# Two attentions, the coupling networks and the flag branch in one program without barriers

## The chip, the cores and the metric

The kernel runs on one core of a Trainium2 chip. Five engines work side by side, each on its own stream of instructions: TensorE (PE, matrix products; its weight loads are listed as PEld), VectorE (DVE), ScalarE (ACT), GpSimd (POOL) and SyncE (SP, which here only issues DMAs). They wait for each other by counting semaphores. The metric is the time of one execution on the device, in microseconds (us); less is better.

## The reference

The input is 4 batches of 1024 tokens with 128 channels. Two layers are computed, each as `x = x + s * silu(g)` on the normalized x. In the first, s is a full attention with 16 heads of 8 channels and g a spiking feed-forward. In the second, s is a causal attention with ALiBi slopes, and g comes from small coupling networks that are applied in three cycles:

```
def _L1_ffn_ref(x, ...):
    gf = _global_net(x.mean(axis=1, keepdims=True), ...)
    out = x
    for _ in range(NUM_CYCLES):                  # 3
        tf = _coupling_net(out, ...)             # 128 -> 128 -> 64 -> 32 -> 1, gelu between, sigmoid at the end
        combined = 0.7 * gf + 0.3 * tf
        coupling = BASE_COUPLING + adaptive_range * (combined - 0.5) * 2.0
        out = out + coupling * _twist(out)
    return out

xn = _layernorm(x)
s = _L1_attn_ref(xn, ...)                        # causal, 16 heads, softmax(q k / sqrt(8) + alibi)
g = _silu(_L1_ffn_ref(xn, ...))
x = x + s * g
```

## The kernel before

**Stages.** `build` calls five stages one after the other: `prologue`, `row_maxima(0)`, `first_attention`, `middle`, `row_maxima(1)`, `second_attention`. Each is a block of its own: at its end every engine drains and meets the others at a barrier, and only then does an engine start on the next block. The blocks also own their tiles: each attention allocates its ring of four tiles `probs` and its PSUM banks (three slots of two banks for scores, one bank `o_ps` for the output, one bank `side`), and `middle` its hidden layers `h1`, `h2`, `h3`, `th` and two groups of four banks, pa and pb.

**The attentions.** A step is 512 queries by 128 keys of four heads. PE makes scores in two units of 128x1024, ACT takes the exponential of each unit into the ring, POOL masks the diagonal pieces (second attention only), and PE multiplies the ring's tile with the values `vt` into `o_ps`. Steps run in pairs. The order on each engine is written out by hand. Between the pairs PE does side work in the bank `side` (a "fill"), by a table: `side_fills` for the first attention and `second_fills` for the second. The second attention has 18 steps for each of 4 batches.

**`middle`.** It runs the coupling networks on all four batches, in two streams (0: batches 0 and 1; 1: batches 2 and 3) that take turns: round n belongs to stream n % 2, and there are six rounds, 0 to 5. In a round PE computes a layer, ACT its Gelu, four layers long; ACT ends with two Tanh (`couple`), and DVE with two twists, `twist(n, 0)` and `twist(n, 1)`, one for each batch of the stream. A twist is three instructions on 1024 columns (two on 64 partitions each, L1517, and one on 128, L1520). In each pass of the loop DVE does `twist(n - 2, 1)` and `twist(n - 1, 0)`. Twist (3,1) below is `twist(3, 1)`.

`middle` also finishes what the first attention left of batch 3, half 1 (the last 512 tokens). In round 0 PE projects the attention's output (L1654), DVE adds and multiplies it (`mix`, L1541) and normalizes (up to L816), PE turns it (L1632). In round 5, the last one, its q and k are projected (L1636, `rows_of`), ACT and DVE split them into a high and a low part, PE makes its v (L1640, `values`), and POOL, PE and DVE its norms (`norm_peak`). From the norms DVE makes `flag`, which says whether scores can grow so large that row maxima are needed. `row_maxima(1)` loads it on SP, PE and DVE (L682, L706, L729) and branches; with these inputs the flag is 0 and the long branch isn't taken.

**Around the seams.** ACT loads its Gelu table at the first instruction of `middle` (L1446) and the Exp table at the last (L1477). DVE clears `o_ps` at the start of each attention, and PE waits for this before its first scores.

## Time and profile before

| | us |
|---|---|
| median of 3 runs | 916.91 (916.01 to 917.1) |
| the profiled execution | 914.3 |
| its span | 912.6 |
| ACT busy | 829.2 (91%) |
| PE busy | 780.9 (86%) |
| DVE busy | 395.0 (43%) |
| POOL busy | 210.3 (23%) |

The span goes from the first to the last instruction of the profiled execution; about 1.7 us lie around it. Instructions are named by their line in the kernel, their engine and the tiles that they write and read. "Idle before, releaser" is the time for which an engine stood still before an instruction, and the engine and line that ended the wait; a name with a q at its end, as PEq, is the engine's sequencer, which handles waits, branches and barriers.

### The profile page before, as it was taken

The numbers are of one execution on the slowest core, as the hardware profiler recorded it, in microseconds if no ns is written. First come the engines' busy times: TensorE is split into PE (matmuls) and PEld (weight loads), VectorE is DVE, ScalarE is ACT, GpSimd is POOL, SyncE is SP. The second block draws the span as 40 slices with busy tenths as digits, with TensorE's granted clock in tenths as the row PEclk, the third lists the DMA queues.
The fourth block names the chain that finished last, engine by engine and source line by source line (L and its number), as shares of the span: only waits on it lengthen the run. The fifth ranks groups of instructions, "written<-read, shape, count | busy, mean of one in ns | idle before, by whom it ended". The sixth has DMA issues, their size and how long they took to land. (4 is left out here: it accounts for less than half of the span.)

```text
span 912.6 us, 22160 instructions
## 1 busy us (share of the span) xinstructions
PE 780.9 (86%) x9374; PEld 305.5 (33%) x9374; DVE 395.0 (43%) x862; ACT 829.2 (91%) x919; POOL 210.3 (23%) x259
## 2 busy tenths in 40 slices
PE   3949999899999999998999988755887878878876
PEld 2412434234343343433334333212332323323322
DVE  7821254443747446474444777881120121121122
ACT  7759999999999999999999956656999999999996
POOL 2201110130202212121311112002234334324333
PEclk9969999999999999999999999986999999999999
DMA  6882020200300202103000034010112022022000
GB/s 181 281 280 38 2 75 3 74 2 3 98 25 18 104 2 75 48 2 121 2 2 24 25 90 168 0 47 1 38 38 86 14 74 86 1 87 86 2 13 24
DMA packets 31948, 53.45 MB, mean 59 GB/s; under 512 B 5480, under 2 KB 16360, under 8 KB 31848
## 3 DMA queue, kind: packets, MB, share of 16 engines
q1 hardware_dynamic: 31848, 52.01, 18.2%
q8 instruction: 75, 1.23, 0.6%
q14 instruction: 25, 0.20, 0.1%
HBM read 31.29 MB, written 20.71 MB: 57 GB/s over the span
## 5 line engine op out<-in xcount | busy, mean ns | idle before, releaser
L979 ACT ACTIVATE a_probs<-a_sc 128x1024 f32<-128x1024 f32 x512 | 473.6, 1035 | 10.0 <-PE a_sc L1178 9.7
L1846 ACT ACTIVATE a_probs<-a_sc 128x1024 f32<-128x1024 f32 x288 | 269.6, 1047 | 21.6 <-PE a_sc L1997 17.1
L1193 PE MATMUL a_o<-a_probs,vt 128*18 128x256 f32 (+1 forms) x3072 | 271.3, 456 | 0.0
L1178 PE MATMUL a_sc<-q_st,k_st 32*128 32x512 f32 x1024 | 130.7, 499 | 29.5 <-ACT a_probs L979 23.4
L2032 PE MATMUL a_o<-a_probs,vt 128*18 128x256 f32 (+3 forms) x1856 | 152.7, 437 | 0.7
L1991 PE MATMUL a_sc<-q_st,k_st 32*128 32x512 f32 (+3 forms) x768 | 78.5, 423 | 62.5 <-ACT a_probs L1846 51.1
L1872 POOL TENSOR_SCALAR_AFFINE_SELECT a_probs<-a_probs 128x512 f32<-128x512 f32 x128 | 82.8, 666 | 189.9 <-ACT a_probs L1846 189.9
L1193 PEld LDWEIGHTS a_o<-a_probs,vt 128*18 128x18 f32 x3072 | 65.2, 97 | 142.9 <-issue 102.7
L1178 PEld LDWEIGHTS a_sc<-q_st,k_st 32*128 32x128 f32 x1024 | 50.6, 183 | 145.4 <-ACT a_probs L979 135.4
L1006 POOL TENSOR_TENSOR early<-early 128x512 f32<-128x512 f32 x32 | 38.4, 1200 | 176.9 <-DVE early L1116 176.9
L1991 PEld LDWEIGHTS a_sc<-q_st,k_st 32*128 32x128 f32 x768 | 37.1, 185 | 123.8 <-ACT a_probs L1846 106.5
L1905 DVE STREAM_TRANSPOSE a_turn<-a_o 128x512 f32<-128x512 f32 x15 | 10.8, 717 | 152.9 <-PE a_o L2032 152.9
L2032 PEld LDWEIGHTS a_o<-a_probs,vt 128*18 128x18 f32 x1856 | 40.6, 97 | 69.4 <-issue 51.2
L1116 DVE TENSOR_SCALAR early<-a_side 128x512 f32<-128x512 f32 x32 | 22.1, 691 | 67.0 <-PE a_side L112 67.0
L1120 DVE TENSOR_SCALAR y<-a_side,rho 128x128 f32<-128x128 f32 x32 | 9.0, 345 | 92.5 <-PE a_side L112 92.5
L992 POOL TENSOR_TENSOR early<-early,y 128x512 f32<-128x512 f32 x7 | 10.6, 1513 | 144.5 <-DVE early L1131 144.5
L1397 ACT ACTIVATE n_h<-n_ps,cn_b 128x1024 f32<-128x1024 f32 (+1 forms) x24 | 24.1, 1006 | 20.5 <-PE n_ps L1585 10.3
L1517 DVE SCALAR_TENSOR_TENSOR early<-n_th,n_offset,y 64x1024 f32<-64x1024 f32 x24 | 30.8, 1285 | 8.6 <-ACT n_th L1418 8.2
L1014 POOL TENSOR_TENSOR a_square<-parts 128x512 bf16<-128x512 f32 x12 | 15.1, 1258 | 82.7 <-DVE parts L1148 82.7
L112 PE MATMUL a_side<-proj_t,early 128*32 128x128 f32 x1024 | 33.8, 273 | 0.0
L112 PE MATMUL a_side<-y,fc_t 128*32 128x512 f32 x256 | 33.3, 592 | 0.0
L112 PEld LDWEIGHTS a_side<-proj_t,early 128*32 128x32 f32 x1024 | 29.3, 110 | 5.8
(236 smaller groups left out, 712.9 us busy)
## 6 DMA issues: line engine op xcount, KB each, us to landing
q_st<-q_hl SPq DMA_DIRECT2D x48, 256.0 KB
k_st<-k_hl SPq DMA_DIRECT2D x48, 256.0 KB
q_hl<-parts SPq DMA_DIRECT2D x12, 512.0 KB, 4.3
k_hl<-parts SPq DMA_DIRECT2D x12, 512.0 KB, 4.5
q_hl<-early SPq DMA_DIRECT2D x4, 512.0 KB, 4.8
k_hl<-early SPq DMA_DIRECT2D x4, 512.0 KB, 5.3
out_dram<-x SPq DMA_DIRECT2D x7, 256.0 KB, 4.3
x<-in_L_attn_x_dram SPq DMA_DIRECT2D x3, 512.0 KB, 5.9
```

The lines of the kernel that those rows point to most:

```text
L112: ins = nc.tensor.matmul(out[c:c + COLUMN, :], weight[:, c:c + COLUMN], rows, start=start, stop=stop, tile_position=(0, c))
L979: nc.scalar.activation(probs[t % RING][:, 2 * pair:2 * pair + 2, :], scores[unit % SLOTS][:, :, :], ACT.Exp).then_inc(expd, 1)
L1006: pool.tensor_tensor(hidden[f], hidden[f], hidden[f], ALU.mult).then_inc(hid_rdy, 1)
L1116: ins = nc.vector.tensor_scalar_max(hidden[hf[1]], side[:, :], 0.0)
L1178: ins = nc.tensor.matmul(scores[(2 * t + i // 2) % SLOTS][:, i % 2, :], k_st[part, g, kt * P:(kt + 1) * P], q_st[part, g, qh * HALF:(qh + ...
L1193: ins = nc.tensor.matmul(o_ps[32 * h:32 * h + 2 * W9, c0:c1], vt[b % 2][:, kt, gp, h, W9 * gs:W9 * gs + 2 * W9], probs[t % RING][:, h, c0: ...
L1397: nc.scalar.activation(out, source, ACT.Gelu, bias=bias[:, 0:1]).then_inc(squashed[z], 1)
L1517: ins = nc.vector.scalar_tensor_tensor(moved[dst, :], t[src, :], offset[src, 2 * z + k:2 * z + k + 1], out[src, :], ALU.add, ALU.mult)
L1846: nc.scalar.activation(probs[t % RING][:, 2 * pair:2 * pair + 2, :], scores[unit % SLOTS][:, :, :], ACT.Exp).then_inc(expd, 1)
L1872: ins = pool.affine_select(out=part, in_=part, compare_op=ALU.is_ge, fill=0.0, base=0, pattern=[[0, G], [1, P]], channel_multiplier=-1)
L1991: ins = nc.tensor.matmul(banks[i][:, at:at + w], k_st[part, 2 * gp + gs, kt * P:(kt + 1) * P], q_st[part, 2 * gp + gs, qh * HALF + q0:qh * ...
L2032: ins = nc.tensor.matmul(o_ps[32 * h:32 * h + 2 * W9, q0:q0 + w], vt[b % 2][:, kt, gp, h, W9 * gs:W9 * gs + 2 * W9], probs[t % RING][:, h, ...
```

## The change

The first attention, `middle`, `row_maxima(1)` and the second attention become one block, `attentions`. Each stage now returns five parts, one for each engine, and the block calls them in turn for each engine; there is no barrier between them. `prologue` and `row_maxima(0)` (now `first_row_maxima`) stay blocks of their own.

- Where the barriers were, engines wait for counts: `attended` holds the counts of the first attention that `middle` waits for, `flagged` the flag's five operations, `drained` the last Tanh, `freed` the two Tanh of round 5, and `twisted` the twists.
- Tiles are shared. The ring of `probs` is one tensor for both attentions; `middle` keeps `h1`, `h2`, `h3` and stream 0's `th` in it, so the exponentials of step 2 of the second attention wait for the last twist of stream 0. The PSUM banks of all stages are the same two groups of four.
- The start of `middle`: PE turns half 0 and does the second part of the first layer before the output projection of half 1.
- The last half batch: q is projected in round 2 and k in round 3, into the fourth bank of the stream. ACT copies each twice (`copy_and_high`), DVE subtracts (`low31`), the norms are made in round 4, and the flag in round 5 after `twist(4, 0)`. Its v is a new fill of the second attention, in pair 3 of batch 0.
- PE and DVE branch before the last two twists, and DVE clears `o_ps` between them. PE's first scores no longer wait for that; its first product does.

The core of the diff:

```diff
+def attentions(nc, a, s, out_t):
+        ring = sb("ring", [P, RING * G, HALF])
+        ps = [ctx.enter_context(nc.psum_tensor(f"c_ps{z}", [P, 4, HALF], F32))[:, :, :] for z in range(2)]
+            "scores": [ps[0][:, 0:2, :], ps[0][:, 2:4, :], ps[1][:, 0:2, :]], "o_ps": ps[1][:, 2, :], "side": ps[1][:, 3, :],
...
+            def _(dve):
+                first_dve(dve)
+                couple_dve(dve)
+                attend_dve(dve)
...
 # middle, ACT
+        def copy_and_high(z):
+            bank = ps[z][:, 3, :]
...
+            nc.scalar.activation(raw[z], bank, ACT.Identity, bias=bias).then_inc(side_act, 1)
+            nc.scalar.activation(parts[1][:, z, 0, :], bank, ACT.Identity, bias=bias).then_inc(side_act, 1)
...
-                    if n == ROUNDS - 1:
-                        high(0, 1, pa[:, 0, :])
                     second_layer(n)
...
-                    if n == ROUNDS - 1:
-                        high(1, 1, pa[:, 1, :])
+            if n in (2, 3):
+                copy_and_high(n - 2)
 # middle, DVE
+        flagged = Chain(dve, peaks)
                 for n in range(2, ROUNDS):
                     twist(n - 2, 1)
+            if n in (3, 4):
+                low31(n - 3)
                     twist(n - 1, 0)
-                low(0, 1, pa[:, 0, :])
-                low(1, 1, pa[:, 1, :])
-                twist(ROUNDS - 2, 1)
-                values(1, pa[:, 2, :])
+            if n == ROUNDS - 2:
                 norm_peak(1, pa[:, 3, :])
                 dve.wait_ge(side_dve, dve_count("n31"))
-                flagged = Chain(dve, peaks)
-                flagged.after(nc.vector.reduce_max(top[:, :], norms[:, :], axis=AX.X))
-                twist(ROUNDS - 1, 0)
+                flagged.mark(nc.vector.reduce_max(top[:, :], norms[:, :], axis=AX.X))
                 dve.wait_ge(peak_turned, 1)
...
+        twist(ROUNDS - 2, 1)
+        room["dve_branch"](dve)
+        twist(ROUNDS - 1, 0)
+        dve.wait_ge(*room["drained"])
+        nc.vector.memset(room["o_ps"], 0.0).then_inc(room["o_clear"], 1)
                 twist(ROUNDS - 1, 1)
 # second attention
+        if b == 0:
+            fill("v", B - 1, 1, 3)
...
+            if t == 2:
+                act.wait_ge(twisted[0], 2 * CYCLES)
...
+                elif unit == SLOTS - 1:
+                    pe.wait_ge(*room["freed"][0])
...
+                if t == 0:
+                    pe.wait_ge(o_clear, 1)
```

In the orders below, y is the state of the coupling networks, xs the normalized half, wo_x the output weights, on the attention's output. PE at the seam from the first attention to `middle`, before:

```order
L1193 MATMUL a_o<-a_probs,vt 18x256 x7
L928 UNCONDITIONAL_BRANCH
L1578 UNCONDITIONAL_BRANCH [waits barrier_Pool_Activation_PE_DVE_SP_release]
L1585 MATMUL n_ps<-y,cn_w 128x512 [waits cn_in]
L1585 MATMUL n_ps<-y,cn_w 128x512
L1654 MATMUL n_ps<-wo_x,on 128x128 x4
L1632 MATMUL n_ps<-ident,xs 128x128 x4
L1585 MATMUL n_ps<-y,cn_w 128x512 x2
```

The same place in the change:

```order
L1212 MATMUL c_ps<-c_ring,vt 18x256 x7
L1625 MATMUL c_ps<-y,cn_w 128x512 [waits a0_expd,a0_side_in,cn_in]
L1625 MATMUL c_ps<-y,cn_w 128x512
L1672 MATMUL c_ps<-ident,xs 128x128 [waits a0_expd,a0_xs1_rdy]
L1672 MATMUL c_ps<-ident,xs 128x128 x3
L1625 MATMUL c_ps<-y,cn_w 128x512 x2
L1701 MATMUL c_ps<-wo_x,on 128x128 [waits a0_on_rdy]
```

The barrier is gone, and the projection, which needs DVE's `on`, stands behind the turn and the whole first layer. DVE at the end of the coupling networks, before, from the norms of the last half on (early and y belong to the twists):

```order
L1494 TENSOR_REDUCE norms<-n_ps 64x1 [waits n_side_ps]
L1569 TENSOR_REDUCE n_top<-norms 64x1 [waits n_side_dve]
L1517 SCALAR_TENSOR_TENSOR early<-n_th,n_offset,y 64x1024 [waits n_squashed1,n_peaks]
L1517 SCALAR_TENSOR_TENSOR early<-n_th,n_offset,y 64x1024
L1520 SCALAR_TENSOR_TENSOR y<-early,n_slope,y 128x1024 [waits n_twist_link]
L1572 COPY n_peak<-n_ps 1x64 [waits n_peak_turned]
...
L1575 TENSOR_SCALAR flag<-n_peak 1x1 [waits n_peaks]
L1517 SCALAR_TENSOR_TENSOR early<-n_th,n_offset,y 64x1024 [waits n_squashed1]
...
L1358 UNCONDITIONAL_BRANCH
L727 UNCONDITIONAL_BRANCH [waits barrier_Pool_Activation_PE_DVE_SP_release]
L729 TENSOR_LOAD flag
```

In the change the flag comes before the last three twists, and the clearing of the output bank between the last two:

```order
L1611 TENSOR_SCALAR flag<-n_peak 1x1 [waits c_flagged]
L1552 SCALAR_TENSOR_TENSOR early<-c_ring,n_offset,y 64x1024 [waits n_squashed0]
...
L1555 SCALAR_TENSOR_TENSOR y<-early,n_slope,y 128x1024 [waits n_twist_link]
L748 TENSOR_LOAD flag [waits c_flagged]
...
L1552 SCALAR_TENSOR_TENSOR early<-c_th,n_offset,y 64x1024 [waits n_squashed1]
...
L1616 MEMSET c_ps 128x512 [waits n_squashed1]
L1552 SCALAR_TENSOR_TENSOR early<-c_th,n_offset,y 64x1024 [waits n_squashed1]
```

## Rows read from the trace of the kernel before

**Rows 1.** Stretches: start:end, length, busy us of each engine, PE's clock, DMA.

```profile
609.60:620.70 11.10, 0.27 (x2) 0.08 (x2) 8.76 (x12) 0.19 (x1) 0.00 (x0) 0.55 0.01 1
...
621.00:640.00 19.00, 13.37 (x132) 5.03 (x132) 1.40 (x3) 15.62 (x17) 4.96 (x8) 0.73 0.00 1
...
656.70:691.60 34.90, 27.64 (x368) 10.49 (x368) 6.03 (x10) 34.67 (x39) 13.34 (x18) 1.00 0.16 50
```

**Rows 2.** Timeline, first seam: start, us, engine, line, operation, idle before and releaser.

```profile
537.81 0.65 DVE L1071 SCALAR_TENSOR_TENSOR y<-ext,y 128x512 f32<-128x512 f32 x1
...
538.75 1.28 ACT L1446 ACT_TABLE_LOAD   x1 [4.52 <-PEq L928]
...
538.79 3.60 PE L1585 MATMUL n_ps<-y,cn_w 128*128 128x512 f32 x4 [3.29 <-PEq L928]
...
541.33 0.16 DVE L1539 TENSOR_SCALAR n_half_b<-cn_scalars 128x2 f32<-128x2 f32 x1
...
542.18 1.15 PE L1654 MATMUL n_ps<-wo_x,on 128*128 128x128 f32 x8
...
543.37 0.69 DVE L1541 TENSOR_TENSOR early<-n_ps,xn 128x512 f32<-128x512 f32 x1 [1.87 <-PE n_ps L1654]
...
549.98 1.12 DVE L816 TENSOR_SCALAR xs<-x,n_moments,n_rstd 128x128 f32<-128x128 f32 x4
...
551.51 0.66 PE L1632 MATMUL n_ps<-ident,xs 128*128 128x128 f32 x4
```

**Rows 3.** PE's branch, both passes: ns min/median/max, first and last start.

```profile
L706 PEldq TENSOR_LOAD <-flag x2: 310/702/1093, 52.0 to 618.5; - x2
...
L706 PEldq COMPARE_BRANCH  x2: 230/238/245, 53.5 to 619.2; - x2
```

**Rows 4.** Timeline of ACT in a steady round.

```profile
574.50 0.69 ACT L1397 ACTIVATE n_h<-n_ps,cn_b 128x512 f32<-128x512 f32 x1 [1.18 <-PE n_ps L1600]
576.40 1.11 ACT L1397 ACTIVATE n_h<-n_ps,cn_b 128x1024 f32<-128x1024 f32 x1 [1.22 <-PE n_ps L1585]
```

**Rows 5.** Timeline from round 5 to the first exponential of the second attention.

```profile
596.57 1.98 PE L1585 MATMUL n_ps<-y,cn_w 128*128 128x512 f32 x4
...
597.86 2.58 DVE L1517 SCALAR_TENSOR_TENSOR early<-n_th,n_offset,y 64x1024 f32<-64x1024 f32 x2 [1.78 <-ACT n_th L1418]
...
599.50 1.12 PE L1636 MATMUL n_ps<-early,w 128*128 128x512 f32 x2
...
601.68 1.11 ACT L1397 ACTIVATE n_h<-n_ps,cn_b 128x1024 f32<-128x1024 f32 x1 [0.33 <-PE n_ps L1592]
...
606.15 2.12 ACT L1418 ACTIVATE n_th<-n_ps,n_half_b 128x1024 f32<-128x1024 f32 x2 [1.49 <-PE n_ps L1613]
...
609.58 0.20 ACT L1477 ACTIVATE n_warm<-n_half_b 128x2 f32<-128x2 f32 x1
...
616.86 1.28 DVE L1520 SCALAR_TENSOR_TENSOR y<-early,n_slope,y 128x1024 f32<-128x1024 f32 x1
...
620.73 0.80 PE L1991 MATMUL a_sc<-q_st,k_st 32*128 32x512 f32 x4 [10.80 <-DVE a_o L1948]
...
621.75 1.94 ACT L1846 ACTIVATE a_probs<-a_sc 128x1024 f32<-128x1024 f32 x2 [11.97 <-PE a_sc L1997]
```

**Rows 6.** Timeline: the first products of the second attention.

```profile
628.75 2.85 PE L2032 MATMUL a_o<-a_probs,vt 128*18 128x512 f32 x16
```

**Rows 7.** Timeline: a tiny DVE operation beside POOL's square; a mask.

```profile
529.66 1.04 DVE L267 SCALAR_TENSOR_TENSOR a_root<-a_fix,a_root 128x4 f32<-128x4 f32 x1
...
623.76 0.64 POOL L1872 TENSOR_SCALAR_AFFINE_SELECT a_probs<-a_probs 128x512 f32<-128x512 f32 x1 [19.23 <-ACT a_probs L1846]
```

**Rows 8.** Timeline: a side fill of 32 products in the second attention.

```profile
682.50 1.06 PE L112 MATMUL a_side<-wo_x,on 128*32 128x128 f32 x32
```

**Rows 9.** The page's groups: busy us, mean ns of one exponential.

```profile
L979 ACT ACTIVATE a_probs<-a_sc 128x1024 f32<-128x1024 f32 x512 | 473.6, 1035 | 10.0 <-PE a_sc L1178 9.7
L1846 ACT ACTIVATE a_probs<-a_sc 128x1024 f32<-128x1024 f32 x288 | 269.6, 1047 | 21.6 <-PE a_sc L1997 17.1
```

## What I expect of the change, and why

> **What bounds the kernel now.** I read the busy time by stretch first. Inside the second attention ScalarE (ACT) is the bound: a full batch has it busy 34.67 of 34.90 us, so work taken from other engines there gives nothing [rows 1]. Between the stages it is otherwise. From 609.60 to 620.70 us ACT is busy 0.19 us of 11.10 and TensorE (PE) 0.27 us, while VectorE (DVE) works 8.76 us: DVE alone finishes the coupling, and nobody may start the second attention [rows 1]. So I went on to the order of time around the two seams. At the first, ACT is free at 538.75 - 4.52 = 534.23 us and PE at 538.79 - 3.29 = 535.50; both resume at 538.75 to 538.79, because DVE settles the last quarter of the batch until 537.81 + 0.65 = 538.46 and a barrier follows [rows 2]. At the second, ACT is done with tables and all at 609.78, DVE twists until 618.14, and the first exponential starts at 621.75 [rows 5].
>
> **First seam: the barrier goes, and what then stands behind it.** With counts in place of the barrier, PE runs the first coupling layer right after its last product. It starts at 535.6 instead of 538.79, and since PE has not rested, I give it 1.98 us (the same layer in a round, row at 596.57 [rows 5]) and not the 3.60 us it takes now at the low clock [rows 2]. ACT's Gelu table load (1.28 us) moves into its own wait. PE's order becomes layer (to 537.6), turn of xs1 (0.66, row at 551.51, to 538.2), second half of the layer (to 540.2), output projection of the last attention half (1.15, to 541.3) [rows 2]. All that is some 4 us earlier than now, but DVE is the next to be late. Its chain of constants runs 538.79 to 541.33 + 0.16 = 541.49 and cannot begin before the gate ends at 538.46: it ends at 541.2. Projection and constants meet there, and DVE's `mix` starts at 541.4 rather than 543.37, 2.0 us sooner [rows 2]. The last normalization is all DVE from there; its last step ends at 549.98 + 1.12 = 551.10 now, so at 549.1. The turn of that half stood behind other PE work until 551.51, and starts at 549.2 in the change: 2.3 us gained. Against it stands one collision: POOL's square of k moves into this chain, and a tiny DVE operation that meets such a square took 1.04 us where its like takes 0.16 [rows 7]: 0.9 us. The Newton steps are a third of the chain, so I take 2.2 us, with 1.4 and 2.4 as ends. SP's 24 DMAs for the seam start sooner as well; their reader is the second attention, 60 us later, and SP's queue holds nothing else then: nothing.
>
> **Rounds 2 to 4: work moved into gaps.** The last half's q and k are made in rounds 2 and 3. On PE one projection each (1.12 us, row at 599.50) comes before the third layer, which waits for ACT's second Gelu anyway. On ACT two copies (0.69 us each, what the third Gelu of the same size takes) follow that Gelu, which ends at 574.50 - 1.18 = 573.32; they end at 574.75 and push the third Gelu by 0.3 us. But ACT is next needed at 576.40, and idled 1.22 us before it: hidden [rows 4]. On DVE one subtraction (about the 0.69 of the `mix`, of the same size [rows 2]) lies in the 1.78 us that it idles before the round's second twist: hidden [rows 5]. In round 4 DVE gets the norm maximum (0.7 by the same row) and the top, which is tiny, between the twists of batches 2 and 3 of stream 1; with links 1.0 us. Twist (3,1), which ends at 597.86 - 1.78 = 596.08 now, ends at 597.1, and the layer behind it, now at 596.57, starts at 597.15. The next twist starts at 597.86 as before [rows 5].
>
> **Round 5 and the second seam.** That layer ends at 599.13 (1.98) and ACT's Gelu of it (1.11) at 600.3. PE's second layer follows at once, where now it stands behind a projection until 600.6; ACT's second Gelu comes at 601.5 instead of 601.68. The third Gelu ends 0.2 sooner than its 606.15 - 1.49 = 604.66, at 604.5; a layer on PE lies 1.2 us between two ACT operations (1.18 and 1.22 [rows 4]) and not 1.49, since `values` no longer stands before it. So the Tanh pair runs 605.7 to 607.85 (now from 606.15), the Exp table until 609.15 and the warm-up (0.20) until 609.4, against 609.78 now [rows 5]. Will the scores be there? PE is free of the coupling at 605.7. It loads the flag and branches: 618.5 to 619.45 in the second pass, 52.0 to 53.75 in the first [rows 3]. DVE makes the flag after PE's tiny product (behind the second layer, at 601.7) and twist (4,0), which ends at 597.86 + 2.58 + 1.28 = 601.75: known at 602.8 with five tiny operations. So scores start by 607.6 and the first unit takes 1.02 us (620.73 to 621.75): 608.6, before 609.4 [rows 5]. The first exponential moves from 621.75 to 609.4, **12.3 us**. The ends: 12.4, and 11.3 if the branch costs PE 1 us more than its first pass showed on top of that slack.
>
> What is late next is DVE. It does twist (4,1) to 606.7, the branch (under 1.6), twist (5,0) to 612, the clearing of the output bank (half a us) to 612.5, twist (5,1) to 616.4. The first product needs the bank; it comes 628.75 - 621.75 = 7.0 us behind the first exponential now, so at 616.4: 3.9 us of cover, so nothing [rows 5, 6]. If that cover went, each us would count.
>
> **Start of the second attention.** Its first 18.25 us hold 15.62 us of ACT work: 2.63 us idle, because PE is at the low clock (0.73 on average, 16 products in 2.85 us) [rows 1, 6]. In the change PE stands still for a us or more at the branch and then does about 1 us in 4 until the products: I take the low clock, and 0 gained. The Trainium skill (TensorE: Matmul & The Clock Gate, "What's actually happening") says that the throttled state is the default and activity releases it. By that the stretch would stay slow as now; the row here at the low clock after a pause agrees, and none shows so sparse a stretch.
>
> **Added: the last half's v as a side fill** in pair 3 of the second attention: 32 small products, 1.06 us on PE in a warm stage [rows 8], where PE has some slack; a DVE addition behind it delays nobody, as the next fill comes three pairs later. PE was 79% busy in a full batch [rows 1]. Ends 0 and 0.9 us; I take 0.4.
>
> **Sum.** 2.2 + 12.3 - 0.4 = 14.1 us. Profiled execution 914.3 (span 912.6) to 900.2; the median of the runs is 2.6 us above the profiled one, so 916.9 - 14.1 = **902.8 us**. By the ends of the terms: 901.8 (2.4 + 12.4 + 0) to 905.1 (1.4 + 11.3 - 0.9).
>
> **Rivals.**
> A, the clock stays up: PE rests under 2 us before the scores, where it had rested 3.29 us before the low-clock layer. Then most of the 2.63 us of ACT idling goes, say 2.1: 900.7. For it: the shorter rest; against: three quarters of the following 9 us are rest too.
> B, masks against twists. POOL's masks of the first steps (0.64 us each, one or two for a step [rows 7]) now meet the last six twist instructions of 1.28 us. If each of the first three masks waits for one, and the products with them, 1.5 to 3 us: 904.3 to 905.8. For it: the 1.04 us row. Against: the first mask has 4 us until its product. The Trainium skill (SBUF — State Buffer, "SBUF: two separate sides") says the pair of ports that DVE and GpSimd share is an exclusive lock, also for a DVE operation with two SBUF inputs beside a GpSimd one that reads SBUF; that speaks against overlapping these stages, and would give this rival's time.
> C, the branch costs more inside one program than between barriers (1 to 3 us on PE beyond its cover): 903.8 to 905.8. For it: the first pass took 1.75 where the second took 0.95. Against: the jump itself is 0.23 to 0.25 us in both [rows 3].
> D, the change does not overlap: some count holds the scores until DVE's last twist, 618.14 less 2.2. Of the 3.6 us from there to the first exponential some 2.5 go, and the first seam's 2.2: about 5 us, 912.
> E, slower than before: the ring of probabilities, written by ACT, masked by POOL and read by PE, now lies in one tensor that also holds the coupling's hidden layers, so every exponential could meet a neighbour at its place. With 800 exponentials it takes 18 ns each (14.1/800) to undo the gain, and 21 ns to be slower by 0.2%: 919. Against: their mean is 1035 and 1047 ns in the two attentions, whose rings lie in different places now, 12 ns apart [rows 9].
>
> **How the numbers follow.** Forecast 0.55, A 0.15, B 0.13, C 0.09, D 0.04, E 0.03; 0.01 for anything near no change. The range takes in forecast, A, B and C with their bounds, from 900 to 906.3. Faster by over 0.2% (1.8 us, about what a measurement of this kernel tells from no change) 0.96, within 0.01, slower 0.03.
>
> **What would show it.** After: the first layer starts within 0.3 us of the last product and lasts about 2 us; the last turn of xs1 is 2.3 us earlier; rounds 2 to 4 keep their length; the first exponential starts near 607.2, directly behind the table load, with ACT's idle before it under 0.5 us and DVE twisting until 614; PE's clock is low for some 10 us after. If rounds 3 and 4 are longer, a gap was too small; if ACT waits for PE after its warm-up, the branch is C; if PE waits for POOL before its first products, it is B. The forecast fails most likely by what the first 20 us of the second attention do.

## The result, and the profile after

The changed kernel takes 904.65 us (median of four runs, 902.61 to 909.48) against 917.0 for the kernel before (four runs, 916.01 to 917.93; the 916.91 of the table before is the median of the first three): a ratio of 0.9873, 95% interval 0.9829 to 0.9917, so 1.3% faster. The forecast was 902.8 us, with 900.0 to 906.3 as its range. The profiled execution is the slowest of the four, 909.48 us with a span of 907.7 us. The same kernel was measured once more as **after_again**, whose profiled execution of 904.25 us lies at its median; its trace is read beside the first.

The first seam in the changed kernel; the columns are start and length in us, engine, line, operation, operands, count, and in brackets the idle time before it and what ended that. These rows answer to [rows 2].

```profile
534.44 1.28 ACT L1479 ACT_TABLE_LOAD   x1
...
535.62 1.98 PE L1625 MATMUL c_ps<-y,cn_w 128*128 128x512 f32 x4
...
541.18 0.69 DVE L1579 TENSOR_TENSOR early<-c_ps,xn 128x512 f32<-128x512 f32 x1
...
546.52 1.01 DVE L263 TENSOR_TENSOR n_fix<-n_fix,n_var 128x4 f32<-128x4 f32 x1
...
549.53 0.66 PE L1672 MATMUL c_ps<-ident,xs 128*128 128x128 f32 x4 [2.31 <-DVE xs L839]
...
551.22 3.61 PE L1625 MATMUL c_ps<-y,cn_w 128*128 128x512 f32 x4
```

The first layer follows the last product at once and takes 1.98 us instead of 3.60; VectorE's mix starts at 541.18 instead of 543.37, and the last turn of xs1 at 549.53 instead of 551.51. That is near the forecast, but not by the steps of the forecast. Its collision, a tiny operation that meets POOL's square of k (here 1.01 us), did not move into this chain: the kernel before has one there already, 0.89 us at 548.66 us (L264), beside POOL's square at 548.50. What is new is a second one, `n_var` at 544.67 us, which takes 0.62 instead of 0.17 us beside POOL's square at 544.23. From the start of `mix` to the end of the last `xs` VectorE needs 8.29 us instead of 7.73. The last line was not forecast: round 1's first layer takes 3.61 us, what round 0's took in the kernel before.

The rounds and the second seam of the changed kernel, in the order of time (answering to [rows 5, 6]):

```profile
555.88 2.11 ACT L1442 ACTIVATE c_ring<-c_ps,n_half_b 128x1024 f32<-128x1024 f32 x2
...
564.45 3.51 PE L1625 MATMUL c_ps<-y,cn_w 128*128 128x512 f32 x4
...
603.79 0.14 DVE L1611 TENSOR_SCALAR flag<-n_peak 1x1 int32<-1x1 f32 x1
...
605.85 2.09 PE L1653 MATMUL c_ps<-c_ring,n_w_all 32*128 32x512 f32 x8 [0.88 <-ACT c_ring L1421]
606.91 1.46 PE L2041 MATMUL c_ps<-q_st,k_st 32*128 32x512 f32 x4
...
607.99 2.12 ACT L1442 ACTIVATE c_th<-c_ps,n_half_b 128x1024 f32<-128x1024 f32 x2 [2.29 <-PE c_ps L1653]
...
611.53 1.92 ACT L1896 ACTIVATE c_ring<-c_ps 128x1024 f32<-128x1024 f32 x2
...
612.68 0.69 PE L2041 MATMUL c_ps<-q_st,k_st 32*128 32x384 f32 x4 [4.13 <-ACT c_ring L1896]
...
616.22 2.39 POOL L1921 TENSOR_SCALAR_AFFINE_SELECT c_ring<-c_ring 128x512 f32<-128x512 f32 x2 [2.05 <-ACT c_ring L1896]
...
618.67 3.19 PE L2084 MATMUL c_ps<-c_ring,vt 128*18 128x512 f32 x16
...
622.69 11.19 ACT L1896 ACTIVATE c_ring<-c_ps 128x1024 f32<-128x1024 f32 x12 [1.98 <-PE c_ps L2041]
```

The first exponential (611.53) stands directly behind the table load and its warm-up, with no wait of its own, 10.22 us earlier than before. The scores (606.91) are there long before. But TensorE's last layer of 605.85 takes 2.09 us for what takes 1.14 in other rounds, and ScalarE waits for it.

The page's groups of the two attentions' exponentials in the changed kernel (busy us, mean ns | idle before), against [rows 9]:

```profile
L1001 ACT ACTIVATE c_ring<-c_ps 128x1024 f32<-128x1024 f32 x512 | 473.5, 1035 | 10.4 <-PE c_ps L1197 10.1
L1896 ACT ACTIVATE c_ring<-c_ps 128x1024 f32<-128x1024 f32 x288 | 269.7, 1046 | 14.3 <-PE c_ps L2041 8.0
```

The exponentials cost what they did. Of the second attention's 21.6 us of idle time only 7.3 are gone, though its first exponential lost its wait of 11.97 us [rows 5]: some 4.7 us of idle time are new.

For the accounting I cut the time at five marks of ScalarE. Two of the kernel before were not shown yet, the first pair of Tanh and the ninth exponential of the second attention:

```profile
556.20 2.11 ACT L1418 ACTIVATE n_th<-n_ps,n_half_b 128x1024 f32<-128x1024 f32 x2
...
632.13 2.85 ACT L1846 ACTIVATE a_probs<-a_sc 128x1024 f32<-128x1024 f32 x3 [1.34 <-PE a_sc L1991]
```

Here are the same marks in after_again, and in **stoke_lean**, the most telling of the experiments below, with some rows of TensorE among them. First after_again:

```profile
555.42 2.11 ACT L1442 ACTIVATE c_ring<-c_ps,n_half_b 128x1024 f32<-128x1024 f32 x2
...
564.00 1.98 PE L1625 MATMUL c_ps<-y,cn_w 128*128 128x512 f32 x4
...
609.45 1.92 ACT L1896 ACTIVATE c_ring<-c_ps 128x1024 f32<-128x1024 f32 x2
...
620.60 4.69 ACT L1896 ACTIVATE c_ring<-c_ps 128x1024 f32<-128x1024 f32 x5 [1.98 <-PE c_ps L2041]
```

Then stoke_lean:

```profile
553.79 2.11 ACT L1448 ACTIVATE c_ring<-c_ps,n_half_b 128x1024 f32<-128x1024 f32 x2
...
602.11 1.14 PE L1659 MATMUL c_ps<-c_ring,n_w_all 32*128 32x512 f32 x8
...
606.85 1.92 ACT L1907 ACTIVATE c_ring<-c_ps 128x1024 f32<-128x1024 f32 x2
...
612.77 2.04 PE L2095 MATMUL c_ps<-c_ring,vt 128*18 128x512 f32 x16
...
615.35 2.86 ACT L1907 ACTIVATE c_ring<-c_ps 128x1024 f32<-128x1024 f32 x3 [0.41 <-PE c_ps L2052]
```

The stretches between the marks, in us of the profiled executions. The first mark is the start of the Gelu table load (in the kernel before the end of the last exponential, 534.23), the third the last round's Tanh pair:

| stretch | before | after | after_again | stoke_lean |
|---|---|---|---|---|
| start to last exponential | 534.23 | 534.44 | 534.08 | 534.02 |
| to the first Tanh (first seam) | 21.97 | 21.44 | 21.34 | 19.77 |
| to the last Tanh (rounds) | 49.95 | 52.11 | 50.48 | 49.52 |
| to the first exponential (second seam) | 15.60 | 3.54 | 3.55 | 3.54 |
| to the ninth exponential | 10.38 | 11.16 | 11.15 | 8.50 |
| to the end of the span | 280.47 | 285.01 | 281.90 | 280.85 |
| span | 912.6 | 907.7 | 902.5 | 896.2 |

The second seam gives 12.05 to 12.06 us in all three. What differs between the changed kernel's own runs, and again between it and stoke_lean, are the rounds, the first exponentials and the stretch behind them.

The granted clock of TensorE is what they differ in. Stretches of the kernel before, the changed kernel and stoke_lean, in this order (start:end, length, busy us of PE, PEld, DVE, ACT, POOL, then PE's clock as a share of 2.4 GHz; the rest is DMA):

```profile
549.00:557.00 8.00, 7.21 (x34) 3.25 (x34) 4.83 (x12) 5.24 (x8) 4.66 (x7) 1.00 0.97 337
557.00:569.00 12.00, 9.89 (x37) 3.64 (x38) 8.97 (x10) 7.25 (x12) 0.00 (x0) 1.00 0.14 54
604.00:624.00 20.00, 4.83 (x34) 2.39 (x34) 14.24 (x18) 6.21 (x7) 0.77 (x2) 0.67 0.12 46
```

```profile
549.00:557.00 8.00, 6.51 (x26) 3.20 (x26) 3.63 (x8) 2.72 (x4) 2.95 (x5) 0.79 0.45 167
557.00:569.00 12.00, 10.21 (x34) 3.36 (x34) 8.64 (x10) 5.72 (x9) 0.00 (x0) 0.86 0.00 0
604.00:624.00 20.00, 11.70 (x76) 4.25 (x76) 12.54 (x10) 13.25 (x15) 4.89 (x6) 0.57 0.00 1
```

```profile
549.00:557.00 8.00, 6.85 (x32) 3.31 (x34) 5.18 (x10) 3.71 (x4) 2.96 (x5) 1.00 0.40 150
557.00:569.00 12.00, 10.83 (x42) 3.57 (x44) 8.94 (x8) 7.96 (x11) 0.00 (x0) 1.00 0.00 0
604.00:624.00 20.00, 16.32 (x175) 7.19 (x175) 11.03 (x12) 19.11 (x22) 6.49 (x8) 1.00 0.00 1
```

By stretches of half a microsecond, the clock of the changed kernel is at 0.5 (1.2 GHz) in 551 to 555, 564.5 to 568.5, 605.5 to 623, 636 to 640, 708 to 712 and 779.5 to 783.5 us. In after_again it is in 549 to 553, 603.5 to 621 and 634.5 to 638 us; the kernel before has 538.5 to 542.5 and 610.5 to 631.5. All have further such stretches in the start-up and at the very end, which this change does not touch.

### The profile page after: what moved, and what is told of

Read it like the earlier page. It is cut to its first block, busy times and chain, and to the rows that moved or that the text cites. A ratio compares the mean times of both kernels' runs of the same rounds, so it can differ in the third digit from the quotient of the medians.

```text
span 907.7 us, 22196 instructions
## 1 busy us (share of the span) xinstructions
PE 788.5 (87%) x9398; PEld 307.3 (34%) x9398; DVE 396.8 (44%) x862; ACT 830.4 (91%) x921; POOL 212.5 (23%) x259
## 3 DMA queue, kind: packets, MB, share of 16 engines
q8 instruction: 76, 1.25, 0.6%
## 4 chain that ended last, share of the span: by engine, by line
PE 69%; ACT 18%; DVE 4%; issue 3%; ACTq 0%; DVEq 0%
PE c_ps L1212 25%; PE c_ps L1197 13%; ACT c_ring L1896 11%; PE c_ps L2084 10%; PE c_ps L112 10%; PE c_ps L2041 7%; ACT c_ring L1001 5%; PE c_ps L1625 2%; DVE early L1552 1%; ACT c_ring L1421 1%; ACT xs L1903 1%; DVE y L1555 1%; PE c_ps L1653 0%; ACT ext L1006 0%; PE c_ps L2047 0%
## 5 line engine op out<-in xcount | busy, mean ns | idle before, releaser
L1001 ACT ACTIVATE c_ring<-c_ps 128x1024 f32<-128x1024 f32 x512 | 473.5, 1035 | 10.4 <-PE c_ps L1197 10.1
L1896 ACT ACTIVATE c_ring<-c_ps 128x1024 f32<-128x1024 f32 x288 | 269.7, 1046 | 14.3 <-PE c_ps L2041 8.0
L1212 PE MATMUL c_ps<-c_ring,vt 128*18 128x256 f32 (+1 forms) x3072 | 271.7, 457 | 0.0
L2084 PE MATMUL c_ps<-c_ring,vt 128*18 128x256 f32 (+3 forms) x1856 | 157.0, 447 | 0.7
L1197 PE MATMUL c_ps<-q_st,k_st 32*128 32x512 f32 x1024 | 131.0, 500 | 29.5 <-ACT c_ring L1001 22.9
L1921 POOL TENSOR_SCALAR_AFFINE_SELECT c_ring<-c_ring 128x512 f32<-128x512 f32 x128 | 83.9, 675 | 200.6 <-ACT c_ring L1896 200.6
L2041 PE MATMUL c_ps<-q_st,k_st 32*128 32x512 f32 (+3 forms) x768 | 80.5, 434 | 53.3 <-ACT c_ring L1896 52.8
L1212 PEld LDWEIGHTS c_ps<-c_ring,vt 128*18 128x18 f32 x3072 | 65.2, 97 | 143.1 <-issue 102.9
L1197 PEld LDWEIGHTS c_ps<-q_st,k_st 32*128 32x128 f32 x1024 | 50.6, 183 | 145.6 <-ACT c_ring L1001 135.4
L2041 PEld LDWEIGHTS c_ps<-q_st,k_st 32*128 32x128 f32 x768 | 37.6, 188 | 116.1 <-ACT c_ring L1896 103.7
L2084 PEld LDWEIGHTS c_ps<-c_ring,vt 128*18 128x18 f32 x1856 | 41.2, 98 | 71.9 <-issue 53.3
L112 PE MATMUL c_ps<-proj_t,early 128*32 128x128 f32 x1024 | 33.8, 273 | 0.0
L112 PE MATMUL c_ps<-y,fc_t 128*32 128x512 f32 x256 | 33.3, 592 | 0.0
```

The lines of the kernel that those rows point to most:

```text
L112: ins = nc.tensor.matmul(out[c:c + COLUMN, :], weight[:, c:c + COLUMN], rows, start=start, stop=stop, tile_position=(0, c))
L1001: nc.scalar.activation(probs[t % RING][:, 2 * pair:2 * pair + 2, :], scores[unit % SLOTS][:, :, :], ACT.Exp).then_inc(expd, 1)
L1197: ins = nc.tensor.matmul(scores[(2 * t + i // 2) % SLOTS][:, i % 2, :], k_st[part, g, kt * P:(kt + 1) * P], q_st[part, g, qh * HALF:(qh + ...
L1212: ins = nc.tensor.matmul(o_ps[32 * h:32 * h + 2 * W9, c0:c1], vt[b % 2][:, kt, gp, h, W9 * gs:W9 * gs + 2 * W9], probs[t % RING][:, h, c0: ...
L1896: nc.scalar.activation(probs[t % RING][:, 2 * pair:2 * pair + 2, :], scores[unit % SLOTS][:, :, :], ACT.Exp).then_inc(expd, 1)
L1921: ins = pool.affine_select(out=part, in_=part, compare_op=ALU.is_ge, fill=0.0, base=0, pattern=[[0, G], [1, P]], channel_multiplier=-1)
```

## Experiments

The theory after the first look: both seams give what was forecast, and part of it is given back because TensorE now rests in new places and its clock falls there. The rivals: VectorE and GpSimd hinder each other where stages now overlap; the v projection or the early flag costs more than thought. "Unread matmuls" are matmuls of one weight block with three others (384 columns), into a PSUM bank that is free at that point; nobody reads them:

```diff
+def stoke(nc, s, bank, n):
+    for _ in range(n):
+        nc.tensor.matmul(bank[:, 0:3 * C], s["w1"][:, 2, :], s["w1"][:, :, :].rearrange("p n c -> p (n c)"), start=True, stop=True)
```

Medians and ratios are against runs of the kernel before on the same chip in the same batch (medians 916.4 to 916.7 us).

**after_again**, the unchanged copy.

> The changed kernel as it is, measured again as the mark for the runs beside it. The theory (both overlaps bring what was forecast, 2.2 us and about 12 us; TensorE's rests let its granted clock fall to 0.5 at places that differ from run to run) expects 903 to 909 us with the mean granted clock between 0.967 and 0.978, a time that falls as that mean rises, and the first exponential of the second attention between 607 and 612 us from the span's start. Were it contention of VectorE and GpSimd instead, the time would not follow the clock.

Measured: 904.43 us (903.01 to 904.68), ratio 0.9864 (0.9845 to 0.9883), clock 0.973 to 0.977. The time, the clock and the first exponential (609.45 us) lie in the expected ranges. That the time falls as the clock rises holds for three of the four (0.973: 904.62; 0.974: 904.25; 0.977: 903.01), not for 904.68 at 0.976. There is one hint more: a later first layer, at the same place and behind the same work, took 3.51 us in the first profile (564.45) and 1.98 here (564.00). Nothing in the program differs; the clock does.

**stoke_all**, many unread matmuls. The expectation miscounts them: the kernel has 28, not 48 (5 ahead of the last turn; 2 ahead of and 2 behind the third layer as listed, but none in round 0; 4; 3+2; 2; 2), and the next text's 45 repeats that.

```diff
@@ coupling, TensorE
         global_layer(0, 2, pb[:, 1, :])
+        stoke(nc, s, pa[:, 0, :], 5)
         turn_in(1)
...
+            if n not in (2, 3):
+                stoke(nc, s, ps[n % 2][:, 2, :], 2)
             third_layer(n)
+            if n in (1, ROUNDS - 1):
+                stoke(nc, s, ps[n % 2][:, 0, :], 2)
...
         pe.wait_ge(squashed[0], squash_count(ROUNDS - 2, "t1"))
+        stoke(nc, s, pa[:, 2, :], 4)
@@ second attention, TensorE
                 score(2 * pair)
+            if pair == 0:
+                pe.wait_ge(*room["freed"][0])
+                stoke(nc, s, scores[2][:, 0, :], 3)
+                pe.wait_ge(*room["freed"][1])
+                stoke(nc, s, side[:, :], 2)
+            if pair == 1:
+                stoke(nc, s, side[:, :], 2)
...
                 score(2 * pair + 1)
+            if pair == 0:
+                stoke(nc, s, side[:, :], 2)
```

> The changed kernel with matmuls added whose results nobody reads (48 in all, three passes' worth of weights as moving data, 384 columns each, about 0.42 us at the full clock), put where TensorE waits: 5 ahead of the last turn of xs1, 2 ahead of the third layer of rounds 0, 1, 4 and 5 and 2 behind it in rounds 1 and 5, 4 behind the last round's final layer, 3+2 behind the first score step of the second attention and 2 each behind the next two. Theory (the clock falls because TensorE rests there): no stretch at 0.5 between 540 and 640 us but those that remain by chance, round 1's first layer 1.98 us instead of 3.61, pairs of tanh at 567.9, 577.5, 587.1, 596.7 or earlier and 1.3 to 1.8 us before those of the changed kernel, time 1 to 3 us below the changed kernel's. Rival (the clock falls whatever TensorE does, or the lost time is VectorE's and GpSimd's): no gain, or 0.5 to 2 us more, since the added matmuls stand ahead of needed ones.

Measured: 908.29 us (907.01 to 908.68), 3.9 us slower than the changed kernel although the clock is higher (0.981 to 0.984). A miss that both theories share in. The clock did what the first expects (1.00 from 540 to 637 us), but the unread matmuls stood in the way. Here are some of them in round 1, and what ScalarE waits for in the second attention's first steps:

```profile
562.58 1.56 PE L1305 MATMUL c_ps<-w 128*128 128x384 f32 x4
...
565.07 1.56 PE L1305 MATMUL c_ps<-w 128*128 128x384 f32 x4
...
617.21 1.94 ACT L1908 ACTIVATE c_ring<-c_ps 128x1024 f32<-128x1024 f32 x2 [2.10 <-PE c_ps L2059]
```

One unread matmul is two instructions and costs 0.70 us (3.49 us for the five ahead of the turn) and not the 0.42 I had estimated. Four of them make the step from the first to the second Tanh pair 13.45 us instead of 11.70, and the five behind the first score step (612.78 to 616.24 us) hold the next one back until ScalarE has waited 2.10 us. This profile also came to the first seam 2.4 us later than after_again, at 536.44 us, behind a start-up with the low clock until 71 instead of 64.5 us, and its clock fell twice behind 637 us. So the run can't decide between clock and contention; fewer unread matmuls were needed.

**stoke_lean**: only what fits into the waits that the rows show (13 unread matmuls; the text says 14 and counts one for round 0, which got none).

```diff
+        stoke(nc, s, pa[:, 0, :], 3)
         turn_in(1)
...
+            if n not in (2, 3):
+                stoke(nc, s, ps[n % 2][:, 2, :], 1)
             third_layer(n)
+            if n == ROUNDS - 1:
+                stoke(nc, s, ps[n % 2][:, 0, :], 1)
@@ second attention, TensorE
+                pe.wait_ge(*room["freed"][0])
+                stoke(nc, s, scores[2][:, 0, :], 2)
+                pe.wait_ge(*room["freed"][1])
+                stoke(nc, s, side[:, :], 2)
+            if pair == 1:
+                stoke(nc, s, side[:, :], 1)
...
+            if pair == 0:
+                stoke(nc, s, side[:, :], 1)
```

> The changed kernel with 14 unread matmuls instead of the 45 of stoke_all (each 0.70 us by that run's rows), only as many as fit into TensorE's waits of the changed kernel: 3 ahead of the last turn of xs1 (2.1 us into 2.31), 1 ahead of the third layer of rounds 0, 1, 4 and 5, 1 behind round 5's, 4 behind the first score step and 1 each behind the next two. In stoke_all the clock stayed at 1.00 from 540 to 637 us, but the added matmuls themselves stood in the way: tanh of round 1 13.45 us behind round 0's instead of 11.70. Theory (clock) expects here the clock of stoke_all without that delay: tanh of round 1 11.7 to 12.4 us behind round 0's, the first exponential at 607 to 610 us, the first sixteen product matmuls 1.7 instead of 3.19 us, and 901 to 903.5 us, so 1 to 3 us below the changed kernel. Rival (the clock costs nothing that ends last; the first steps wait for VectorE and GpSimd): 904 to 906 us.

Measured: 898.6 us (897.05 to 902.94), ratio 0.9810 (0.9786 to 0.9834): 5.8 us below the changed kernel's 904.43, twice what I had expected. By the ratios, 0.9810 against 0.9864, it is 4.9 us, and their intervals do not meet. The clock stays at 1.00 from 65.5 to 891 us. By the table of stretches it gains 1.57 us in the first seam, 0.96 in the rounds, 2.65 up to the ninth exponential and 1.05 after it, against after_again; the last layer takes 1.14 us instead of 2.09 and the first sixteen products 2.04 instead of 3.19. Counted from the first exponential, VectorE's twists stand at the same places and take the same time. GpSimd's masks come up to 1.05 us earlier, as the exponentials do, and the one that meets a twist takes 1.29 us where it took 0.81. So contention did not become less. That settles the main question: work that nobody reads, put into TensorE's rests, shortens the kernel, and what it changes ahead of the instructions that got shorter is the clock.

**small_masks**, the rival of contention by itself. It leaves out most of the mask of the first four steps.

```diff
+                width = 4 if t < 4 else P
-                part = probs[t % RING][:, :, n * P:(n + 1) * P]
+                part = probs[t % RING][:, :, n * P:n * P + width]
```

> The changed kernel with GpSimd's causal masks of the first four steps of the second attention shrunk from 128 to 4 columns, so that they neither take time nor stand beside VectorE's last twist (this leaves part of the first scores unmasked, so the output is another). In the changed kernel the masks of 616.2 us took 2.39 us instead of 1.23 beside the twist, the twist 2.87 and 1.54 instead of 2.58 and 1.28, and the first product began 0.44 us behind a mask. The rival of contention expects 1 to 2.5 us less than the changed kernel's 904.4. The theory of the clock expects 0 to 0.6 us, with the first sixteen product matmuls still at about 3.2 us.

Measured: 904.47 us (903.82 to 909.08), ratio 0.9879 (0.9859 to 0.9900): the changed kernel's own time. Its rows:

```profile
613.88 1.42 POOL L1922 TENSOR_SCALAR_AFFINE_SELECT c_ring<-c_ring 128x16 f32<-128x16 f32 x2 [2.46 <-ACT c_ring L1896]
...
616.33 3.19 PE L2085 MATMUL c_ps<-c_ring,vt 128*18 128x512 f32 x16
...
620.35 11.19 ACT L1896 ACTIVATE c_ring<-c_ps 128x1024 f32<-128x1024 f32 x12 [1.98 <-PE c_ps L2042]
```

With masks of 16 elements a partition, VectorE's last twist is back at 2.58 and 1.28 us (2.87 and 1.54 beside the whole masks). Yet the products still take 3.19 us and ScalarE still waits 1.98 us, 11.14 us behind its first exponential. The collision is real and hidden. Two such small masks beside the twist took 1.42 us, where two others took 0.39. The first of the two took 0.22 us as elsewhere and the second 1.25; it ended 0.08 us behind the twist's instruction that stood beside it. That looks like an operation that waits, and not like one that runs slower. The Trainium skill (SBUF — State Buffer, "SBUF: two separate sides") says that the pair of ports shared by VectorE and GpSimd is an exclusive lock; these rows agree with it.

**seam1_closed**, the first overlap undone.

```diff
         pe.wait_ge(*attended["slots"][1])
+        pe.wait_ge(*attended["gated"])
         first_layer(0, 0)
```

> The changed kernel with the first seam closed again: TensorE's first layer of the coupling networks also waits for the first attention's last gate (538.65 us). The forecast's term for the first seam (2.2 us, 1.4 to 2.4) expects the last turn of xs1 no later than now, because that hangs on VectorE, so the direct loss is in the order of the matmuls: first layer at 538.7 instead of 535.62, output projection at about 542.7, VectorE's mix at 543.7 instead of 541.18, and the whole 2.0 to 2.6 us slower than the changed kernel. If the first seam were worth nothing (hidden behind VectorE's constants): within 0.5 us.

Measured: 908.54 us (904.64 to 914.11), ratio 0.9906 (0.9880 to 0.9931): 4.1 us slower than the changed kernel in the medians, not 2.0 to 2.6. The interval of the ratio just touches that of the changed kernel (up to 0.9883), so the size is not settled. The profiled run is the slowest one:

```profile
541.73 3.05 PE L1625 MATMUL c_ps<-y,cn_w 128*128 128x512 f32 x4 [3.11 <-DVE y L1091]
...
548.55 0.69 DVE L1579 TENSOR_TENSOR early<-c_ps,xn 128x512 f32<-128x512 f32 x1 [4.36 <-PE c_ps L1702]
...
556.91 1.12 PE L1672 MATMUL c_ps<-ident,xs 128*128 128x128 f32 x4 [2.30 <-DVE xs L839]
```

It starts 3.0 us late for reasons of its start-up (table load at 537.38 us). From there the turn of xs1 comes at 19.53 us instead of 15.09, 4.4 us later: TensorE rests 3.11 us, works its first layer and the first turn at the low clock (3.05 instead of 1.98 us, 1.06 instead of 0.60), and VectorE waits 4.36 us for the projection. In this execution the overlap is thus worth the wait and the rest's cost in clock together. The six runs span 9.5 us, in the order of their mean clock (0.969: 914.11; 0.970: 912.16; 0.971: 909.40; 0.973: 907.68; 0.976: 905.51; 0.977: 904.64).

**seam2_closed**, the second overlap undone, save the early flag and the missing barrier.

```diff
+        pe.wait_ge(twisted[1], 2 * CYCLES)
         for pair in range(LAST):
             if 2 * pair < S:
                 score(2 * pair)
```

> The changed kernel with the second seam partly closed: TensorE's first score of the second attention waits for the last twist (about 618.1 us) instead of only for banks. The forecast's term for the second seam (12.3 us, of which about 7.8 us lie between the first exponential at 611.5 and a score that starts at 618.1) expects the first exponential at about 619 to 620 and a time 7 to 9 us above the changed kernel's. Rival (ScalarE would have waited in the first steps of the second attention anyway, for products and masks that need the last twist): 2 to 5 us.

```profile
617.71 1.94 ACT L1896 ACTIVATE c_ring<-c_ps 128x1024 f32<-128x1024 f32 x2 [7.01 <-PE c_ps L2047]
```

Measured: 912.36 us (911.34 to 915.54), ratio 0.9958 (0.9945 to 0.9972): 7.9 us slower than the changed kernel, inside the expected 7 to 9. The first exponential waits 7.01 us behind the warm-up, at 617.71 us (expected 619 to 620; VectorE's last twist ended at 616.62 us in this run, and not at 618.1). The first eight exponentials then take 11.17 us, where after_again has 11.15, so no other wait of the first steps became shorter in its place. Counted from the last Tanh pair, the first exponential comes 10.65 us behind it instead of 3.54.

**flag_late**, one part undone: norms, peak and flag of the last half batch behind the last round.

```diff
@@ coupling, VectorE
-            if n == ROUNDS - 2:
-                norm_peak(1, pa[:, 3, :])
...
         twist(ROUNDS - 2, 1)
+        norm_peak(1, pa[:, 3, :])
...
         twist(ROUNDS - 1, 0)
+        dve.wait_ge(peak_turned, 1)
@@ coupling, TensorE
-            if n == 4:
-                norms_of(1, pa[:, 3, :])
...
         last_layer(ROUNDS - 1)
         pe.wait_ge(squashed[0], squash_count(ROUNDS - 2, "t1"))
+        norms_of(1, pa[:, 3, :])
```

> The changed kernel with one part undone: the last half batch's norms, their peak and the flag are made behind the last round, as in the kernel before, while the two attentions and the rounds stay in one program. The forecast took the early flag as what the second attention's overlap hangs on. With this order the norms' matmuls start at about 610.3 us, the flag follows at about 615 us and the first score at about 615 to 617 us, so the first exponential at 616 to 618 instead of 609.5 to 611.5 us: 5 to 8 us slower than the changed kernel, 909.5 to 912.5 us. If the flag's place were worth little: under 2 us.

```profile
613.53 0.14 DVE L1612 TENSOR_SCALAR flag<-n_peak 1x1 int32<-1x1 f32 x1
...
615.77 1.94 ACT L1891 ACTIVATE c_ring<-c_ps 128x1024 f32<-128x1024 f32 x2 [4.47 <-PE c_ps L2042]
```

Measured: 908.61 us (906.18 to 909.16), ratio 0.9902 (0.9884 to 0.9919): 4.2 us slower than the changed kernel. The first exponential comes at 615.77 us, 4.24 us behind that of the first profile, which had the same first Tanh pair to 0.1 us. The estimate of 5 to 8 us was too high: the flag came at 613.5, not at 615 us. Counted from the last Tanh pair, the first exponential comes 8.10 us behind it instead of 3.54: of the second seam's 12.06 us the early flag is worth 4.56.

**v_late**, the v projection of the last half batch at pair 12 instead of 3.

```diff
-        if b == 0:
-            fill("v", B - 1, 1, 3)
...
+        if b == 0:
+            fill("v", B - 1, 1, 12)
```

> The changed kernel with the v projection of the last half batch (TensorE 1.06 us for its 32 matmuls) moved from the second attention's pair of steps 3 to pair 12, among full steps. The forecast charged it 0.4 us (0 to 0.9) since it stands in the diagonal steps' stretch, where ScalarE waits for TensorE. It expects 0 to 0.9 us less than the changed kernel if that price holds, and no difference where ScalarE is full anyway (the same price at the new place).

Measured: 906.02 us (903.89 to 907.9), ratio 0.9880 (0.9859 to 0.9900), 1.6 us more than the changed kernel, with intervals of the ratios that overlap; at like clock (0.974) it is 906.10 against 904.25. So pair 3 is no worse a place than pair 12. The traces show more. From the ninth exponential of the second attention to the 25th it is 15.58 us without a fill there (kernel before, v_late) and 15.58 with it (stoke_lean); from the 49th to the 57th, around pair 12, it is 7.32 us with the fill (v_late) and 7.32 without (stoke_lean). The fill costs ScalarE nothing at either place. What the profile of v_late has more than stoke_lean's behind the ninth exponential are two waits, together 2.79 us, where the clock fell (775 and 847 us).

**constants_early**, VectorE's constants in the first attention, the projection ahead of the first layer's second half.

```diff
@@ first attention, VectorE
+            if b == 2 and r == 3:
+                room["constants"](dve)
@@ coupling, TensorE
         turn_in(0)
-        first_layer(0, 1)
         pe.wait_ge(*attended["on_rdy"])
...
+        first_layer(0, 1)
         second_layer(0, 0)
```

> The changed kernel with VectorE's fifteen operations on constants (538.83 to 541.27 us, 2.4 us) moved into the first attention, and the output projection of the last half batch ahead of the second half of round 0's first layer on TensorE. The forecast took the chain from the last transpose of the first attention over VectorE's gate, mix and norm to the last turn of xs1 as the one that sets the rounds' start, and the constants as part of it. It expects the mix at about 539.2 instead of 541.2 us, the last turn 2.0 us earlier, and 902 to 903 us in all, 1.5 to 2.2 us below the changed kernel. Rival (TensorE's own order or the clock sets the start): under 0.7 us.

```profile
538.74 0.69 DVE L1587 TENSOR_TENSOR early<-c_ps,xn 128x512 f32<-128x512 f32 x1 [0.51 <-PE c_ps L1708]
...
547.39 0.66 PE L1680 MATMUL c_ps<-ident,xs 128*128 128x128 f32 x4 [0.97 <-DVE xs L839]
```

Measured: 902.43 us (898.57 to 903.13), ratio 0.9841 (0.9819 to 0.9862), 2.0 us less than the changed kernel, with intervals of the ratios that overlap. Its profiled execution is the fastest of the five, 898.57 us, so the rows flatter it. Counted from the table load the mix starts 1.8 us earlier and the turn 1.5. The first Tanh pair gains 3.0 us (18.31 instead of 21.34), more than the turn: TensorE's wait ahead of the turn shrinks from 2.31 to 0.97 us, and the clock does not fall behind it. It falls at the second seam as before (602.5 to 617 us).

**early_and_lean** and **early_and_lean2**, both means together; the second has 1 instead of 3 unread matmuls ahead of the turn, and 2 instead of 1 behind the second score step.

> constants_early and stoke_lean together. If both effects are real and lie at different places, 899 to 901.5 us, which would beat the changed kernel by 3 to 5 us; if the added matmuls fill a wait that the moved constants shorten, 901 to 903 us.

> early_and_lean with 1 instead of 3 unread matmuls ahead of the last turn of xs1 (they stood there 2.1 us in a wait of 0.97 us, which constants_early's rows show), and 2 instead of 1 behind the second score step, since the clock fell at 610.0 to 614.5 us in that run. With the turn at 547.4 us and the clock kept, it expects tanh of round 0 at about 552.1 us from the span's start instead of 553.4, the first exponential at about 605.1 and 896.5 to 898.5 us, 0.5 to 2.5 us below early_and_lean and stoke_lean. If what is left of the spread is the clock of the start-up (47 to 65 us) and of the end, 898 to 899.5 us.

Measured: 899.24 us (897.77 to 901.67), ratio 0.9813 (0.9792 to 0.9834), and 897.27 us (896.29 to 902.93), ratio 0.9810 (0.9783 to 0.9836). The first lies in the range of its first case by its time, but its rows show the mechanism of the second: the first Tanh pair stands 19.27 us behind the table load, against 18.31 in constants_early and 19.77 in stoke_lean, so the three unread matmuls overfill the shortened wait and eat most of the moved constants' gain. The second version has the lowest median: 7.2 us below the changed kernel in the medians, span 894.8 us in its profile, first Tanh pair at 552.32 and first exponential at 605.39 us. By ratios it can't be told from stoke_lean. Its six runs fall into two groups, four at 896.3 to 897.8 us with a clock of 0.986 to 0.989 and two at 902.6 and 902.9 with 0.978; in the only trace the clock is at 1.00 from 64 to 890 us. Where the two slower ones lost theirs no trace shows.

**before_stoked**: unread matmuls in the kernel before.

```diff
@@ first attention, end of TensorE's part
+                pe.wait_ge(expd, 2 * S)
+                stoke(nc, s, scores[0][:, 0, :], 2)
@@ coupling, TensorE, ahead of the turn of the peaks and behind it
+                pe.wait_ge(squashed[1], squash_count(ROUNDS - 1, "t0"))
+                stoke(nc, s, pb[:, 0, :], 3)
...
+                stoke(nc, s, pa[:, 0, :], 10)
@@ second attention, TensorE, behind each of the first three score steps
+                    if pair == 0:
+                        stoke(nc, s, scores[2][:, 0, :], 1)
...
```

> The kernel before, with unread matmuls in TensorE's waits: 2 behind the first attention, 3 ahead of the turn of the peaks, 10 behind it, and 1 each behind the first three score steps. It asks how much of the clock's loss was there before the change. The kernel before showed two such stretches here (538.7 to 542 and 610.3 to 630.8 us): if kept at full clock, its first layer takes 1.98 instead of 3.60 us and its first products 1.5 to 1.7 instead of 2.85 us. Theory (the change opened new rests, so it lost more to the clock than the kernel before did): a gain of 1 to 3.5 us over the kernel before, less than the 5.8 us that the same means gave the changed kernel. Rival (both lose the same): 5 to 6 us.

Measured: 915.87 us (914.05 to 919.47), ratio 1.0000 (0.9986 to 1.0013): no gain at all, less than the theory's 1 us. Its rows at the second seam:

```profile
619.22 0.80 PE L2002 MATMUL a_sc<-q_st,k_st 32*128 32x512 f32 x4 [4.15 <-DVE a_o L1959]
...
620.01 1.61 PE L251 MATMUL a_sc<-w 128*128 128x384 f32 x2
...
627.91 2.46 PE L2043 MATMUL a_o<-a_probs,vt 128*18 128x512 f32 x16
```

The first seam's layer ran at the full clock here (1.96 us instead of 3.60). At the second seam TensorE still rested 4.15 us from the last of the ten to the first score, across the barriers and the branch, where this version has no unread matmul. Its clock was low again from 619 to 629.5 us, and each unread matmul behind the scores cost 1.61 us, ahead of needed ones. In the profile the first Tanh pair comes 20.27 us behind the last exponential instead of 21.97, a gain of 1.70 us. It is spent again: 0.28 us in the first eight exponentials (10.66 instead of 10.38) and 0.92 behind them, where the clock is low from 660 to 664 us, which the profile of the kernel before does not have. Its mean clock is 0.973 to 0.980, above the 0.969 to 0.977 of the kernel before, and the time is the same, so a higher mean clock alone does not make a program faster. These 18 unread matmuls at these places give the kernel before nothing. That it lost less to the clock than the changed kernel is not shown, since the clock was kept in part only, and neither is what fillers between its blocks would do.

## Why the forecast was near, and where its steps were off

**First seam, forecast 2.2 us.** Right in size up to the last turn: counted from the end of the first attention, it came 15.09 us later instead of 17.28, a gain of 2.19. That two errors cancelled in it was luck: `mix` came 2.40 us sooner and not 2.0, and VectorE's chain from there was 0.56 us longer, 0.45 of it by the second collision. The gain had to reach ScalarE's first Tanh pair, and there 0.53 us (after) and 0.63 us (after_again) were left. The step that failed is not one of the sum's but one that is missing: the forecast ended its working at the turn. With VectorE's chain the one to wait for, as forecast, TensorE waited 2.31 us ahead of the turn and its clock then fell to 0.5, at 549 us in after_again (turn 1.11 instead of 0.66 us, last layer 2.09 instead of 1.14) and at 551 us in the first profile (next layer 3.61 instead of 1.98). stoke_lean, with this wait filled, has 19.77 us against the 21.97 of the kernel before: 2.20, the whole gain of the turn.

**Rounds 2 to 4, forecast as hidden.** Nearly. ScalarE's two copies, VectorE's subtraction and norm operations fit; the round with the second pair of copies went from 9.61 to 9.77 us, so 0.16 us showed. Round 5 was to be 0.45 us shorter; in stoke_lean it is 0.60 (8.84 instead of 9.44), but in the changed kernel it is 0.35 longer (9.79). With the projections gone from round 5, TensorE is busy 7.64 of the 10 us ahead of its last layer, where it was busy 9.84, and the layer ran at the low clock. The forecast had not weighed that. The thinner round alone does not decide it: v_late has the same 7.64 us and the layer in 1.14. Over all rounds 0.43 us were gained in stoke_lean, and -0.53 us (after_again) or -2.16 us (after) in the changed kernel itself. The low clock on the last layer costs 0.95 (2.09 instead of 1.14) and, in the run that had it, on round 1's layer 1.53 (3.51 instead of 1.98).

**Second seam, forecast 12.3 us,** of which 11.9 were the distance from the last Tanh pair to the first exponential and the rest round 5. The distance measured 12.05 to 12.06 us in the three profiles of the table. The branch cost nothing that shows (rival C): scores stand at 606.91 us, right behind the last layer, 4.6 us before the exponential. VectorE twisted until 618.1 us, and the first product (618.67) had the bank and the masks by then. flag_late and seam2_closed show what the parts are worth when undone: 4.2 and 7.9 us in the medians, 4.56 and 7.11 us by the rows.

**Start of the second attention, forecast 0.** The low clock was rightly expected, but not for its reason. TensorE did not rest at the branch: the scores follow the last layer, ahead of which the clock had already fallen (between 605.5 and 606 us). Its rest of 4.13 us came behind the first score step. The first eight exponentials took 11.15 us instead of 10.38: 0.77 us lost. The alternative, rival A with 2.1 us more, was rightly priced: 1.88 us in stoke_lean (8.50 instead of 10.38). It did not come by itself. The Trainium skill (TensorE: Matmul & The Clock Gate, "What's actually happening"), which the forecast set beside this, says that activity releases the throttle; stoke_lean's rows agree (clock 1.00 from 604 to 624 us with TensorE busy 16.32 us of them, 0.57 in the changed kernel with 11.70).

**v as a side fill, forecast 0.4.** It cost nothing. In stoke_lean the stretch behind the ninth exponential is 280.85 us against 280.47, 0.38 more, but not by the fill. Where it stands, the steps are as long as before: from the ninth exponential to ScalarE's next other operation it is 24.90 us in the kernel before (from 632.13) and in stoke_lean (from 615.35):

```profile
657.03 0.63 ACT L1853 ACTIVATE a_th<-y 128x512 f32<-128x512 f32 x1
```

```profile
640.25 0.63 ACT L1914 ACTIVATE xs<-y 128x512 f32<-128x512 f32 x1
```

From the ninth to the last exponential it is 270.89 and 270.82 us. The difference comes behind that, where the clock is low at the very end and the last projection takes 1.23 instead of 0.71 us. In the changed kernel the stretch behind the ninth exponential is 1.43 (after_again) and 4.54 us longer (after), because the clock fell after the seam too, once and three times; each time ScalarE waits 1.2 to 1.4 us. In the first profile another 0.50 us lie behind the last exponential. One of its three waits:

```profile
639.70 1.02 ACT L1896 ACTIVATE c_ring<-c_ps 128x1024 f32<-128x1024 f32 x1 [1.35 <-PE c_ps L2041]
```

**The sum.** The forecast's 14.1 us were what the change is worth at the full clock, less nothing for the clock. By profiled executions the changed kernel gained 10.1 us (after_again: 0.15 from the start, 0.63 - 0.53 + 12.05 - 0.77 - 1.43) or 4.9 us (after), by medians 12.35. That the median of 904.65 lies only 1.85 us above the forecast is in part luck. I added 2.6 us because the median of the kernel before lay that much above its profiled execution, which is faster than each of its four timed ones (914.3 against 916.01 to 917.93). For the changed kernel after_again's profiled execution lies at the median. By these two profiles the terms were 4.0 us too high, and the 2.6 took back about 2.4; by the medians they were 1.75 too high. Which is nearer, two executions can't show. Two slips of the working change nothing: the ends 2.4 + 12.4 give 902.1 and not 901.8, and 919 us is 20 ns for each exponential and not 21. Rival E (dearer exponentials) fell: 1035 and 1046 ns against 1035 and 1047. Rival B is real as a collision and worth nothing (small_masks). Rival D fell with the first exponential at 611.53.

## What to carry to other kernels

When a barrier goes, follow the gain to the engine that sets the end, not only to the instruction that starts earlier. The engine that ran ahead now waits in a new place, and if it is TensorE, its next instructions may run at half speed. Look in each new wait for the granted clock behind it. If it falls, either shorten the wait (the constants moved out of the chain) or fill it, and fill it only with what fits into the idle time that the rows show, since 28 of these matmuls instead of 13 made the kernel 9.7 us slower here (908.29 against 898.6). And compare the medians with more than one profiled execution: two profiles of one program lay 5.2 us apart.

## What was not expected of the hardware

- The clock of TensorE fell behind a wait of 2.31 us with TensorE busy 12.66 of the 15 us before it (534 to 549 us), as the timeline of the first seam and the granted clock show. The forecast had weighed only the rest of 3.29 us and those at the branch and behind it.
- Whether it falls at a given place varies between executions of one program: the same layer took 3.51 us in one and 1.98 in the next. Among runs of one program the time roughly follows the mean granted clock: 914.1 us at 0.969 to 904.6 at 0.977 for seam1_closed, and two groups, 902.6 to 902.9 at 0.978 and 896.3 to 897.8 at 0.986 to 0.989, for early_and_lean2.
- Thirteen matmuls that nobody reads, by the 0.70 us of one an estimated 9.1 us of work, make the kernel 5.8 us faster in the medians.
- A GpSimd operation on 16 elements a partition took up to 1.4 us for two beside a VectorE operation with two SBUF inputs, and 0.39 us away from it.
